# Spectral matrices loaded and split on half the partitions, the other half filled by a transfer inside SBUF

## What is computed

```python
x = x + _L0_conv_ref(_ln_c(x), L0_conv_kernel_base)
t = _to_tokens(x)
t = t + _L0_ffn_ref(_ln_t(t), L0_ffn_router_w, L0_ffn_router_b, L0_ffn_expert_w, L0_ffn_expert_b)
x = _from_tokens(t, x)
x = x + _L1_conv_ref(_ln_c(x), L1_conv_kernels)
t = _to_tokens(x)
t = t + _L1_ffn_ref(_ln_t(t), L1_ffn_router_w, L1_ffn_router_b, L1_ffn_expert_w, L1_ffn_expert_b)
x = _from_tokens(t, x)
```

```python
Xf = jnp.fft.fftn(X, axes=(1, 2), norm='forward')
r2 = f1[:, None] ** 2 + f2[None, :] ** 2
kernel = kernel_base[r2]
Ym = jnp.einsum('xyij,bxyj->bxyi', kernel, Xm)
Yf = Yf.at[:, idx1[:, None], idx2[None, :], :].set(Ym)
return jnp.fft.ifftn(Yf, s=(S1, S2), axes=(1, 2), norm='forward').real
```

## Time and profile before

| | us |
|---|---|
| median of 3 runs | 950.04 (947.3 to 951.19) |
| the profiled execution | 950.36 |
| its span in the trace | 948.6 |
| PE busy in the span | 843.6 (89%) |
| DVE busy | 774.1 (82%) |
| POOL busy | 570.8 (60%) |
| ACT busy | 506.6 (53%) |

### The profile page before, as it was taken

How to read it: one execution, slowest core, us unless ns; L and a number is a source line. 1 busy time by engine, 2 the same in 40 slices (tenths; PEclk the granted TensorE clock), 3 DMA queues, 4 the chain that set the end, 5 groups by cost and what they waited for, 6 DMA issues and landing times.

```text
span 948.6 us, 23667 instructions
## 1 busy us (share of the span) xinstructions
PE 843.6 (89%) x9122; PEld 689.8 (73%) x9122; DVE 774.1 (82%) x1429; ACT 506.6 (53%) x1051; POOL 570.8 (60%) x504
## 2 busy tenths in 40 slices
PE   6996887687999998995999999999568999999998
PEld 6996867455667666663999999999546666667665
DVE  5758897878999999999777766765787899998884
ACT  2468594794766675202444444443278566676411
POOL 3781204077889887794844434420226888889888
PEclk9997568897999999998999999999859999999999
DMA  9944900205778776774687787787000010101111
GB/s 377 358 106 122 376 3 2 53 1 216 299 285 321 299 292 273 285 294 173 234 282 270 245 291 262 260 285 242 1 1 24 23 46 24 45 24 46 46 42 48
DMA packets 48288, 163.04 MB, mean 172 GB/s; under 512 B 9424, under 2 KB 9936, under 8 KB 46032
## 3 DMA queue, kind: packets, MB, share of 16 engines
q1 hardware_dynamic: 48208, 161.96, 47.0%
HBM read 93.46 MB, written 68.49 MB: 171 GB/s over the span
## 4 chain that ended last, share of the span: by engine, by line
PE 48%; DVE 33%; POOL 6%; issue 5%; ACT 4%; DMA 3%; SPq 1%; POOLq 0%; DVEq 0%; ACTq 0%
PE pair L1732 23%; DVE R L926 11%; PE pair L1659 5%; PE pair L1645 5%; PE pair L1646 4%; DMA X<-x_rows 3%; PE pair L1656 3%; DVE R L866 3%; POOL R L589 3%; DVE R L678 2%; PE pair L1623 2%; DVE work L678 2%; DVE R L855 2%; DVE R L765 2%; ACT pair L1270 1%
## 5 line engine op out<-in xcount | busy, mean ns | idle before, releaser
L926 DVE TENSOR_TENSOR R<-pair,R 128x896 f32<-128x896 f32 x256 | 275.3, 1083 | 43.7 <-PE pair L1646 42.5
L589 POOL TENSOR_TENSOR R<-R 128x768 f32<-128x768 f32 x128 | 231.8, 1811 | 88.1 <-DVE R L926 77.6
L1732 PE MATMUL pair<-R 128*128 (+4 forms) x2880 | 227.1, 242 | 9.7 <-DVE R L1004 9.2
L1732 PEld LDWEIGHTS pair<-R 128*128 128x128 f16 x2880 | 224.0, 98 | 12.9 <-issue 10.4
L1270 ACT ACTIVATE pair<-X,work 128x64 f32<-128x64 f32 x480 | 166.6, 394 | 98.4 <-DVE R L866 95.9
L1645 PE MATMUL pair<-work,R 128*128 128x448 f16 x512 | 186.6, 364 | 22.3 <-DVE R L926 20.5
L1646 PE MATMUL pair<-work,R 128*128 128x448 f16 x512 | 185.8, 363 | 0.0
L599 POOL TENSOR_TENSOR R<-R 128x512 f32<-128x512 f32 x128 | 164.7, 1286 | 10.0
L1019 DVE COPY R<-R 128x1152 f32<-128x1152 f32 x64 | 92.6, 1446 | 65.7 <-PE pair L1732 65.0
L1388 ACT COPY R<-R 128x1152 f32<-128x1152 f32 x64 | 81.9, 1283 | 117.3 <-PE pair L1732 117.3
L1659 PE MATMUL pair<-R,ident_sb 128*128 128x256 f32 x496 | 128.6, 382 | 0.0
(11 more groups left out here) (137 smaller groups left out, 1275.7 us busy)
## 6 DMA issues: line engine op xcount, KB each, us to landing
taps_halves<-R SPq DMA_DIRECT2D x128, 458.5 KB, 3.4
R<-taps_halves SPq DMA_DIRECT2D x64, 917.0 KB, 4.7
X<-x_tok SPq DMA_DIRECT2D x4, 2048.0 KB, 16.6
out<-X SPq DMA_DIRECT2D x15, 512.0 KB, 2.6
R<-spec_pairs SPq DMA_DIRECT2D x16, 272.0 KB, 4.3
X<-x_rows SPq DMA_DIRECT2D x4, 1024.0 KB, 10.8
R<-x_chan SPq DMA_DIRECT2D x4, 1024.0 KB, 13.8
X<-x_rows SPq DMA_DIRECT2D x2, 2048.0 KB, 27.2
```

The costliest lines, as they stand in the source:

```text
L589: pool.tensor_tensor(pr[:, :, 192:384], pr[:, :, 0:192], pr[:, :, 192:384], ALU.add).then_inc(half_ready, 1)
L926: dve.tensor_tensor(pr.rearrange("p t (e c) -> p t e c", c=C), pair[p % 2][:, :].rearrange("p (t e c) -> p t e c", t=2, c=C)[:, :, 0:NE - ...
L1732: mm = pe.matmul(acc[:, y0:y1, x0:x1, :], blocks[i % 2][:, ks, 2 - y, 1 - x, :], src[:, y0 + y:y1 + y, x0 + x:x1 + x, :], start=(ks == 0 a ...
```

## The change

Raw matrices are loaded once, to partitions 0 to 63. ACT and DVE make the halves there alone, one instruction each a step. Then SP issues a DMA from SBUF to SBUF that moves the whole buffer of both halves (64 partitions x 8576 bytes, 549 KB) to partitions 64 to 127, 64 columns further on; the zeros beside the matrices on the lower partitions travel along and land where zeros belong, and the first 64 columns on the upper partitions keep the memset's zeros. PE waits for this transfer instead of for DVE. The rings of raw and split buffers have four places instead of three. POOL clears them with four memsets of 128 x 2176, behind units 20, 24, 28 and 31. SP issues four loads up front, then per step: wait for `k_low`, the transfer, and the load for step t+4. In DVE's stream the rows 0 to 3 stand at unit 31 of stage 1 and behind units 7, 10 and 13 of stage 2, with row t+4 behind bank t.

```diff
-        k_row = [f16(R1, 2304 + 2176 * i, 2176).rearrange("p (s b o) -> p s b o", s=2, b=17) for i in range(3)]
-        k_raw = [R1[:, 8832 + 1088 * i:8832 + 1088 * (i + 1)].rearrange("p (b o) -> p b o", b=17) for i in range(3)]
+        k_raw = [R1[0:64, 2304 + 1088 * i:2304 + 1088 * (i + 1)].rearrange("p (b o) -> p b o", b=17) for i in range(4)]
+        k_flat = [f16(R1, 6656 + 2176 * i, 2176) for i in range(4)]
+        k_row = [m.rearrange("p (s b o) -> p s b o", s=2, b=17) for m in k_flat]
...
         def k_in_count(t):
-            return 32 * (t // 3 + 1)
+            return 16 * (t // 4 + 1)
...
+            def load_pairs(t):
+                sp.dma_start(k_raw[t % 4], spec_pairs[:, PER_STEP * t:PER_STEP * t + PER_STEP, :]
+                             ).then_inc(k_in[t % 4], 16)
+
+            sp.wait_ge(c_dft, 13)
+            for t in range(4):
+                load_pairs(t)
             for t in range(NSTEP):
-                if t < 3:
-                    sp.wait_ge(c_dft, 20 + 2 * t)
-                else:
-                    sp.wait_ge(k_low, 2 * (t - 2))
-                for r in BLOCKS:
-                    sp.dma_start(k_raw[t % 3][r], spec_pairs[:, PER_STEP * t:PER_STEP * t + PER_STEP, :]
-                                 ).then_inc(k_in[t % 3], 16)
-                if t == 5:
+                sp.wait_ge(k_low, t + 1)
+                row = k_flat[t % 4]
+                sp.dma_start(row[64:128, 64:4352], row[0:64, 0:4288]).then_inc(k_shifted[t % 4], 16)
+                if t + 4 < NSTEP:
+                    load_pairs(t + 4)
+                if t == 1:
                     wait_c_dft_low(sp, 32)
                     sp.dma_start(raws_at[0], experts0).then_inc(raw_in, 16)
...
-                if n == 18:
-                    pool.wait_ge(c_dft, 16)
-                    pool.memset(R1[:, 2304:6656], 0.0).then_inc(zeros_ready, 1)
-                if n == 24:
-                    pool.wait_ge(c_dft, 20)
-                    pool.memset(R1[:, 6656:8832], 0.0).then_inc(zeros_ready, 1)
+                if n in (20, 24, 28, 31):
+                    i = (20, 24, 28, 31).index(n)
+                    pool.wait_ge(c_dft, 18 + 4 * i)
+                    pool.memset(k_flat[i].bitcast(F32), 0.0).then_inc(zeros_ready, 1)
...
+            def row_low(t):
+
+                r = BLOCKS[0]
+                row = k_row[t % 4]
+                dve.wait_ge(k_high, t + 1)
+                dve.scalar_tensor_tensor(out=row[r, 1, :, r], in0=k_raw[t % 4], scalar=SCALE, in1=row[r, 0, :, r],
+                                         op0=ALU.mult, op1=ALU.subtract).then_inc(k_low, 1)
...
                 if n == 31:
-                    row_low(0, (0,))
+                    row_low(0)
             h_dft_low_part(3)
             c_dft_low_part(31)
-            row_low(0, (1,))
             for n in range(4, 16):
                 h_dft_low_part(n)
-                if n in (8, 11):
-                    row_low(1, (n // 11,))
-            row_low(2)
+                if n in (7, 10, 13):
+                    row_low(1 + (7, 10, 13).index(n))
...
                 mixed_low_part(t)
-                if t + 3 < NSTEP:
-                    row_low(t + 3)
+                if t + 4 < NSTEP:
+                    row_low(t + 4)
...
+            def row_high(t):
+
+                if t < 4:
+                    act.wait_ge(zeros_ready, t + 1)
                 else:
-                    act.wait_ge(stepped, t - 2)
-                act.wait_ge(k_in[t % 3], k_in_count(t))
-                for i in parts:
-                    r = BLOCKS[i]
-                    act.mul(k_row[t % 3][r, 0, :, r], k_raw[t % 3][r], SCALE).then_inc(k_high, 1)
+                    act.wait_ge(stepped, t - 3)
+                act.wait_ge(k_in[t % 4], k_in_count(t))
+                r = BLOCKS[0]
+                act.mul(k_row[t % 4][r, 0, :, r], k_raw[t % 4], SCALE).then_inc(k_high, 1)
...
-                if n in (29, 30):
-                    row_high(0, (n - 29,))
+                if n == 30:
+                    row_high(0)
             for n in range(4, 16):
                 h_dft_high_part(n)
-                if n in (6, 9):
-                    row_high(1, (n // 9,))
-            row_high(2)
+                if n in (5, 8, 11):
+                    row_high(1 + (5, 8, 11).index(n))
...
                 mixed_high_part(t)
-                if t + 3 < NSTEP:
-                    row_high(t + 3)
+                if t + 4 < NSTEP:
+                    row_high(t + 4)
...
             for t in range(NSTEP):
-                pe.wait_ge(k_low, 2 * t + 2)
-                row = k_row[t % 3]
+                pe.wait_ge(k_shifted[t % 4], k_in_count(t))
+                row = k_row[t % 4]
```

More of the change, by code:

```diff
@@ L189, in metaformer @@
         zeros_ready = sem("zeros_ready")
-        k_in = [sem(f"k_in{i}") for i in range(3)]
+        k_in = [sem(f"k_in{i}") for i in range(4)]
+        k_shifted = [sem(f"k_shifted{i}") for i in range(4)]
         last_in = sem("last_in")
@@ L757, in last_low_part @@
                                          op0=ALU.mult, op1=ALU.subtract).then_inc(last_low, 1)
-            def row_low(t, parts=(0, 1)):
-                raw, row = k_raw[t % 3], k_row[t % 3]
-                for i in parts:
-                    r = BLOCKS[i]
-                    dve.wait_ge(k_high, 2 * t + i + 1)
-                    dve.scalar_tensor_tensor(out=row[r, 1, :, r], in0=raw[r], scalar=SCALE, in1=row[r, 0, :, r],
-                                             op0=ALU.mult, op1=ALU.subtract).then_inc(k_low, 1)
+            def row_low(t):
[4 more added lines that the diff above has]
+                                         op0=ALU.mult, op1=ALU.subtract).then_inc(k_low, 1)
             unit_stats(0, 0, 32)
@@ L1183, in last_high_part @@
                 act.mul(k_last[:, 0], last_raw, SCALE).then_inc(last_high, 1)
-            def row_high(t, parts=(0, 1)):
-                if t < 3:
-                    act.wait_ge(zeros_ready, 1 if t < 2 else 2)
-                else:
-                    act.wait_ge(stepped, t - 2)
-                act.wait_ge(k_in[t % 3], k_in_count(t))
-                for i in parts:
-                    r = BLOCKS[i]
-                    act.mul(k_row[t % 3][r, 0, :, r], k_raw[t % 3][r], SCALE).then_inc(k_high, 1)
+            def row_high(t):
+                if t < 4:
+                    act.wait_ge(zeros_ready, t + 1)
+                else:
+                    act.wait_ge(stepped, t - 3)
+                act.wait_ge(k_in[t % 4], k_in_count(t))
+                r = BLOCKS[0]
+                act.mul(k_row[t % 4][r, 0, :, r], k_raw[t % 4], SCALE).then_inc(k_high, 1)
             act.wait_ge(rank_in, 16)
```

## The result

| | us |
|---|---|
| kernel before, median of 12 runs | 949.59 (947.3 to 953.24) |
| changed kernel, median of 12 runs | 952.93 (950.53 to 956.07) |
| ratio | 1.0033, 95% interval 1.0016 to 1.0049 |
| profiled execution of the changed kernel, its span | 956.0, 954.2 |

The forecast was 947.4 with a range of 944.0 to 952.5. The time lies just above the range and on the other side of the old one.

What follows compares the result with a forecast made beforehand. PE bounds stage 1, DVE stage 2; in stage 3 PE waits 2.22 us for a row and 4.60 for its program. Transposes 3.1 us earlier, less 0.5, gain 2.6: 950.36 becomes 947.8, median 947.4, range 944.0 to 952.5.

Steps and rivals of the forecast that it cites:

- PE waits for its program at crossings of 128 matmuls: Stage 3, kernel before: three holes on a grid of 256 instructions are waits for PE's program, 4.60 us.
- Stage 1 costs nothing: Stage 1: POOL's four memsets stay covered by PE's unbroken work to 67.3; without cover 1.9 us.
- Stage 2, 1.2 us earlier: Stage 2, bound by DVE: mixing starts at 81.2, 1.2 us earlier; bounds 0.7 later to 2.7 earlier.
- The wait for row 3 (2.22 us) goes: Stage 3, step 3: row 3 lands by about 86, before PE arrives at 86.7, so the 2.22 us wait goes.
- Row 4 lands at 91.9: Stage 3, step 4: issue plus 4.5 us landing; PE waits about 1.8 us, step 4 starts 1.4 us earlier.
- Steps 5 to 7 are hidden: Stage 3: rows 5 to 7 are there by 98.2 while `mix_edge` keeps PE busy until 98.3.
- `mix_edge` in 4.7 us: Stage 3, after step 4 begins: 4.7 us in the sum for the end of mixing without holes, 102.9.
- The program's pages, 1.0 and 2.4 us: Crossings at matmuls 527 and 655: holes of 1.0 and 2.4 us, so transposes start at 106.3 instead of 109.47.
- A: Rival: the program's holes close, transposes start at about 103.1, 5.0 us gained, 945.0; chance 0.18.
- B: Rival: the transfer lands late, L = 7.4, transposes at 110.0, no worse than 950.5; chance 0.20.
- C: Rival: transfers of rows 4 to 7 queue and hold PE in steps 5 to 7; 956 at 6 us each; chance 0.07.
- The gain after the transposes: After the first transpose: 0.5 us of the 3.1 given back to the slow clock, leaving a gain of 2.6.

Runs made afterwards that it cites:

- hybrids: Changed kernel with the transfer for rows 0 to 3 only, rows 4 to 7 loaded and split as before: 950.14 us; with `x_tok` also held back 942.05 us.

## Why the prediction was wrong, by its own steps

The failed step is the price of the transfer: its landing time L was taken as 4.5 us and was 6.9 to 9.7 from the third transfer on, and its time on the DMA engines, which PE's program needs too, was put at nothing. The forecast had the first transpose at 106.3, and it came at 114.98, 8.7 us later: 1.7 at step 4 (the landings), 5.6 by longer holes at the crossings behind it (8.97 us against 3.4), and 1.3 by the matmuls there (12.39 against 11.05). By step:

- *PE waits for its program at crossings of 128 matmuls.* Right, and shown: in the kernel before the holes go when `x_tok` goes.
- *Stage 1 costs nothing.* Right: PE was busy 31.30 of 31.30 us up to 67.3, with four memsets beside it.
- *Stage 2, 1.2 us earlier.* Right in sign, measured 1.73.
- *The wait for row 3 (2.22 us) goes.* This failed. Row 3's transfer was issued at 79.87 and landed in 9.7 us; PE waited 1.46 for it, and 1.37 for row 2's before it, where I had "none ahead of step 3". I had it split by 81 and there by 86, five microseconds for a transfer by itself. I also overlooked that the change moves the experts' load (532 KB) from 86.39 to 76.40, in front of rows 2 and 3: in the hybrids, which issue it behind them, these landed in 5.9 and 8.0 to 8.1 us instead of 6.9 and 9.7. Single traces differ by as much, so the load's own share isn't shown.
- *Row 4 lands at 91.9.* It was issued a microsecond earlier than I had it, and step 4 began at 93.62. The landing time L is the term that was mis-sized: 4.5 taken, 7.4 as the upper end, 7.8 at the median, 9.7 at most. The rows for it were single transfers or a pair. I took the price of one into an idle queue and never added up what eight of them and their loads bring: 549 + 278 KB a step at 215 GB/s is 3.8 us of full DMA engines, while rows 0 to 3 were issued 2.8 us apart on the mean (71.33 to 79.87). Rows 4 to 7 bring no load, 2.6 us each at an issue every 2.5 us, but they stand behind that backlog. In all, eight transfers, four loads and the experts' are 6.04 MB, an estimated 28 us at 215 GB/s; the trace has 31.4 from the first issue (71.33) to the last landing (102.7). As the argument against a late landing I wrote that nothing else fills the queues from 87 to 94. The transfers themselves did, with a share of 1.01.
- *Steps 5 to 7 are hidden.* PE waited for no transfer there, but because the pages made it later still: row 7 was there at 102.7 and not at 98.2.
- *`mix_edge` in 4.7 us.* Too short. By the earlier trace rows, 374 matmuls in 11.22 us with the first 105 at 31 ns leave 7.96 us for a stretch for which the sum has 7.1; 192 at 31 ns would be 5.9. The forecast was 0.9 to 1.2 us too early by this alone.
- *The program's pages, 1.0 and 2.4 us.* Measured 3.60, 2.55 and 2.52, and 1.21 at the two crossings ahead. This follows from the same error: I priced the transfer for the engine that waits for it, and not for the other users of its queue. It is the largest term of the balance, +5.28. Of it 0.83 arose ahead of `x_tok`, with only transfers and loads in the queue; the rest, with 3.60 at matmul 399, came with both in the queue.
- *The rivals.* A (the holes close) happened only where the queues were emptied. B had the late landing at 7.4 but left the pages alone, and so came out at 950.5. C had the right quantity, transfers that queue: it decides when the last of them lands after 102.3 (3.6 us each in its sum), and row 7's landed at 102.7 (3.7 each). But it let the transfers hold PE directly, in steps 5 to 7, which happened in steps 2 to 4, and it got 0.07 against rows of a write from 128 partitions, which is not this transfer's shape. The Trainium skill's rule on 64 partitions (SBUF — State Buffer, "Door 1: The DMA port swizzle"), put beside the sum as 0.3 us of landing, was worth more as a rate, times the number of transfers.
- *The gain after the transposes.* The difference at the first transpose, 5.51, is that of the spans, 5.6; the allowance of 0.5 had nothing to act on.

## What to carry to other kernels

A DMA has two prices: its landing, which its waiter pays, and its time on the DMA engines, which everyone behind it pays. Add up the second over the stage before the first is believed: bytes per step over the rate for that shape, against the time per step. And when an engine in a long unrolled stream stalls with no releaser, count instructions between the stalls: if they lie 256 apart, as here, it is most likely waiting for its program; look whether a piece on the instruction queue stands ahead of each hole's end. Moving a big load that nobody needs yet was worth 2.5 us here in the old kernel and 8.1 in the hybrid.

## What the runs showed of the hardware that I had not expected

- PE's program can be the bound of a stage. With the DMA engines full, 128 pairs of weight load and matmul (3.9 to 4.0 us of work) come every 6.4 to 7.6 us: starts at 94.50, 102.07, 108.56 and 114.98 in the changed kernel. The Trainium skill (Runtime: NRT & Kernel Launch, "Instruction fetch mechanics") says a crossing is mostly hidden; here that held with free queues, and with full ones up to 4.97 us were not hidden.
- The cover is thin. In the run without the transfer the pieces at 86.38, 90.09 and 93.60 come about 1 us after PE passed matmuls 143, 271 and 399 (an estimate from 29.4 ns for each), and where PE did wait, in any run, it went on 2.3 to 3.0 us after a piece. That is 3.3 to 4.2 us for a page against some 3.8 of work, if a page is asked for when the one before it is entered.
- SBUF to SBUF between two halves of the partitions: 1.7 us fixed and about 215 GB/s, an estimate from 3.0 us for 270 KB and 4.3 for 549 KB in idle queues; with a row of such transfers the engines were fully busy (1.01) at 220 GB/s.
- Full engines say nothing on bytes: a share of 1.0 went with 206 GB/s (96 to 98 us of the changed kernel, transfers) to 442 GB/s (102 to 104 of the kernel before, `x_tok`), by what filled it.
